# Causal mask of an attention stage moved from TensorE matmuls to GpSimd selections, and expert scatters issued between later gathers

## The reference

```python
xn = _layernorm(x)
x = x + L0_attn(xn, ...) + L0_ffn(xn, ...)          # block 0
xn = _layernorm(x)
x = x + L1_attn(xn, ...) + L1_ffn(xn, ...)          # block 1, a scan over segments of 32

# L0_attn: 16 heads of 8, no mask, scores scaled and multiplied by exp(-1e-4 |i - j|)
attn = softmax(clip(q k^T * scale) * decay); out = (attn v) Wo

# L0_ffn: a causal attention and a mixture of experts
scores = (rope(q) rope(k)^T) / sqrt(8)
scores = where(tril, scores, -inf)
x = x + (softmax(scores) v) w_o
logits = rmsnorm(x) @ w_router; top 2 of 8 experts; each expert keeps its 160 largest gates
xe = xf[tok]                                        # (8, 160, 128), gathered rows
ye = (relu(xe w1) w2) * gates
y = zeros.at[tok].add(ye)                           # rows added back
```

## Time and profile before

| | |
|---|---|
| three runs | 3370.74, 3374.51 (median), 3388.30 us |
| profiled execution | 3378.05 us, of which the profile's span is 3376.2 us |
| busy in the span | PE 2890.8 us, DVE 2501.5, ACT 1930.5, POOL 1697.3 |
| attend, from its first score matmul to its last division | 320.1 to 1525.1 us |
| experts, first gather issued | 1763.95 us |
| expert 0: transposition on PE starts, `ye` done on DVE | 1773.42, 1778.94 us |
| experts, last scatter issued | 1843.30 us |
| preparation of block 1 starts | 1851.1 us |

### The profile page before, as it was taken

One profiled execution on the slowest core, in us unless ns is written; L12 is line 12 of the kernel. 1 busy time (PEld: TensorE's weight loads), 2 busy tenths in 40 slices (PEclk: granted clock), 3 DMA queues, 4 the chain that ended last, 5 costly groups with the idle time before them and its releaser, 6 DMA issues. The chain is left out here.

```text
span 3376.2 us, 133974 instructions
## 1 busy us (share of the span) xinstructions
PE 2890.8 (86%) x56049; PEld 1694.1 (50%) x56049; DVE 2501.5 (74%) x7471; ACT 1930.5 (57%) x3909; POOL 1697.3 (50%) x1600
## 2 busy tenths in 40 slices
PE   5675999999999999997233299999999999999998
PEld 2332333333333333336222167676677767676776
DVE  4567788887888888866660678788888788787876
ACT  4564778787787878772000155555555555555553
POOL 4663000000000000003016499999999999898996
PEclk9777899999999999998565599999999999999999
DMA  3467333333233333309201200000000000000000
GB/s 123 169 207 231 70 83 85 89 77 87 75 85 84 87 87 76 87 25 286 82 27 29 74 4 11 11 11 11 11 11 11 11 11 11 10 7 9 11 7 11
DMA packets 179424, 210.31 MB, mean 62 GB/s; under 512 B 28608, under 2 KB 140288, under 8 KB 178560
## 3 DMA queue, kind: packets, MB, share of 16 engines
q1 hardware_dynamic: 176256, 200.31, 21.3%
q0 software_dynamic: 2560, 1.35, 0.4%
HBM read 125.17 MB, written 75.63 MB: 59 GB/s over the span
## 5 line engine op out<-in xcount | busy, mean ns | idle before, releaser
L778 ACT ACTIVATE at_pA<-at_ps 128x512 f32<-128x512 f32 x1024 | 569.1, 608 | 131.6 <-DVE at_ps L831 131.1
L840 DVE CUSTOM_DVE_ANT_0 at_junk<-at_ps,w_cmask 128x512 f32<-128x512 f32 (+3 forms) x1024 | 462.7, 488 | 169.9 <-PE at_ps L682 169.9
L658 POOL CAST at_mrow<-at_neg 16x128 bf16<-16x128 f32 x64 | 18.0, 282 | 1110.3 <-DVE at_neg L803 1110.3
L831 DVE TENSOR_TENSOR at_ps<-at_ps,w_ratio 128x128 f32<-128x128 f32 (+3 forms) x1024 | 490.4, 493 | 67.2 <-PE at_ps L676 67.0
L784 ACT ACTIVATE at_pB<-at_ps 128x512 f32<-128x512 f32 (+1 forms) x768 | 395.9, 538 | 77.3 <-PE at_ps L692 76.8
L2099 ACT ACTIVATE sc_ee<-sc_ps 128x512 f32<-128x512 f32 x256 | 153.0, 598 | 497.9 <-PE sc_ps L1955 496.5
L676 PE MATMUL at_ps<-at_aq,at_ak 72*128 72x512 bf16 x1024 | 355.9, 391 | 3.5 <-DMA at_ak<-parts_scratch 3.1
L1919 POOL TENSOR_TENSOR sc_rb<-sc_rb,v_sin 128x512 f32<-128x512 f32 x256 | 327.0, 1278 | 48.5 <-DVE sc_ra L2143 48.1
L682 PE MATMUL at_ps<-at_bk,at_bq 72*128 72x512 bf16 (+3 forms) x1024 | 273.2, 309 | 52.3 <-DMA at_bk<-parts_scratch 31.6
L1955 PE MATMUL sc_ps<-sc_xT,v_wqkv 128*128 128x512 f32 x512 | 293.1, 655 | 18.8 <-DVE sc_ra L2143 16.6
L689 PE MATMUL at_ps<-at_bq,at_bk 75*128 75x512 bf16 (+3 forms) x1024 | 283.3, 303 | 18.3 <-DVE at_mx L840 17.3
(11 more groups left out here) (315 smaller groups left out, 6377.9 us busy)
## 6 DMA issues: line engine op xcount, KB each, us to landing
parts_scratch<-fr_parts SPq DMA_DIRECT2D x64, 384.0 KB, 4.1
at_bq<-parts_scratch SPq DMA_DIRECT2D x192, 96.0 KB
at_bk<-parts_scratch SPq DMA_DIRECT2D x192, 96.0 KB
at_aq<-parts_scratch SPq DMA_DIRECT2D x192, 96.0 KB
at_ak<-parts_scratch SPq DMA_DIRECT2D x192, 96.0 KB
v_scratch<-fr_v SPq DMA_DIRECT2D x32, 352.0 KB, 4.3
at_v<-v_scratch SPq DMA_DIRECT2D x32, 352.0 KB, 3.5
parts_scratch<-fr_parts SPq DMA_DIRECT2D x32, 256.0 KB, 3.9
```

The lines of the kernel that those rows point to most:

```text
L778: act.activation(pA[:, n % A_RING, j * S:(j + 1) * S], src, ACT.Exp).then_inc(exped, 1)
L831: dve.tensor_tensor(src[:, 0:wide], src[:, 0:wide], W["ratio"][:, S - wide:S], ALU.mult).then_inc(tilted, 1)
L840: ins = dve.tensor_tensor_reduce(junk[:, P * j * (j + 1) // 2:P * (j + 1) * (j + 2) // 2], src[:, col:col + wide], W["cmask"][:, S - wide: ...
```

## The change

`attend`: the mask matmuls are gone, and each T block is one matmul. GpSimd instead zeroes the future keys in `pB` after the exponentials, with two in-place `affine_select` per head: one over the diagonal square of block 3 when T1's exponential is done, one over those of blocks 0, 1 and 2 (three squares, 384 columns) when T2's is done. A select keeps an entry where column - partition >= 0 and writes 0 elsewhere. PV of a T group waits for the semaphore `cut` of these instead of for `exped`. The splitting of the maxima stays on GpSimd, now in one stream with the selections.

`experts`: GpSimd issues the gathers of experts 0, 1, 2, then the scatters of expert 0, the gathers of 3, the scatters of 1, and so on; the scatters of 6 and 7 come last.

`fold_weights`: `cmaskT` isn't loaded, and two casts to bf16 are gone.

```diff
@@ fold_weights
-                 (W["ident"], c["ident"]), (W["hsum"], c["hsum"]), (cmaskT, c["cmaskT"]),
+                 (W["ident"], c["ident"]), (W["hsum"], c["hsum"]),
...
-            dve.tensor_copy(W["ident_bf"][:], W["ident"][:])
-            dve.tensor_copy(W["cmaskT"][:], cmaskT[:])
@@ attend, gpsimd
-                for n in range(GROUPS):
+                def split_max(n):
                     b = n % 2
                     pool.wait_ge(job_read, jseq["MT", "M", n] + 1)
...
+                def cut_future(n):
+
+                    probs = pB[:, n % T_RING]
+                    pool.wait_ge(exped, nth["exped", ("T1", n)])
+                    lone = probs[:, B_AT[3]:B_AT[3] + P]
+                    pool.affine_select(lone, lone, [[1, P]], ALU.is_ge, 0.0, base=0, channel_multiplier=-1).then_inc(cut, 1)
+                    pool.wait_ge(exped, nth["exped", ("T2", n)])
+                    three = bass.AP(probs.tensor, probs.offset, [list(probs.ap[0]), [S, 3], [1, P]])
+                    pool.affine_select(three, three, [[0, 3], [1, P]], ALU.is_ge, 0.0, base=0, channel_multiplier=-1).then_inc(cut, 1)
+
+                for e in range(STEPS):
+                    n = head_of("T", e)
+                    if n is not None:
+                        cut_future(n)
+                    if e % 4 == 0 and 0 <= e // 4 - 1 < GROUPS:
+                        split_max(e // 4 - 1)
+
@@ attend, tensor
                     for j, col in T_BLOCKS[kind]:
-                        pe.matmul(ps[:, BANK[kind], col:col + S - j * P], bk[:, slot, n % 4, j * P:(j + 1) * P], bq[:, slot, n % 4, j * P:S],
-                                  start=True, stop=False)
-
-                        ins = pe.matmul(ps[:, BANK[kind], col:col + P], W["ident_bf"][:], W["cmaskT"][:], start=False, stop=True)
+                        ins = pe.matmul(ps[:, BANK[kind], col:col + S - j * P], bk[:, slot, n % 4, j * P:(j + 1) * P], bq[:, slot, n % 4, j * P:S],
+                                        start=True, stop=True)
...
-                        pe.wait_ge(exped, nth["exped", (last_head[kind], 4 * g + 3)])
+                        if a == 0:
+                            pe.wait_ge(exped, nth["exped", ("A2", 4 * g + 3)])
+                        else:
+                            pe.wait_ge(cut, 2 * (4 * g + 3) + 2)
@@ experts, gpsimd
+            def fetch(e):
+                for m in (2 * e, 2 * e + 1):
+                    pool.indirect_dma_start(xe[0:HALF, m, :], None, c["xf_d"].rearrange("b s d -> (b s) d"),
+                                            bass.IndirectOffsetOnAxis(rows[0:HALF, m, 0:1], 0)).then_inc(fetched[e], 16)
...
+            def give_back(e):
                 pool.wait_ge(scaled, e + 1)
-
-                pool.wait_ge(summed, 32 * e)
...
+                if e:
+                    pool.wait_ge(summed, 32 * e)
+                for m in (2 * e, 2 * e + 1):
+                    pool.indirect_dma_start(c["h_d"].rearrange("b s d -> (b s) d"),
+                                            bass.IndirectOffsetOnAxis(rows[0:HALF, m, 0:1], 0), ye[0:HALF, m, :], None,
+                                            compute_op=ALU.add).then_inc(summed, 16)
+
+            for e in range(E):
+                fetch(e)
+                if e >= 2:
+                    give_back(e - 2)
+            for e in range(E - 2, E):
+                give_back(e)
```

More of the change, by code:

```diff
@@ L67, in fold_weights @@
         wqkv, wqkv_g, g1 = sb("fw_qkv", [P, 3 * D]), sb("fw_qkv_g", [P, 3 * D]), sb("fw_g1", [P, 1])
-        wq, cmaskT = sb("fw_q", [P, D]), sb("fw_cmaskT", [P, P])
+        wq = sb("fw_q", [P, D])
         ps = ctx.enter_context(nc.psum_tensor("fw_ps", [P, 4, 512], F32))
@@ L501, in attend @@
         pv, ot_cp, job, job_read, m_ready = (sem(n) for n in "pv ot_cp job job_read m_ready".split())
-        v_step, p_step, ones = (sem(n) for n in "v_step p_step ones".split())
+        v_step, p_step, ones, cut = (sem(n) for n in "v_step p_step ones cut".split())
         BANK = dict(A0=2, A1=4, A2=0, A3=1, M0=5, M1=4, M2=3, T0=5, T1=3, T2=2)
@@ L568, in attend @@
         LAST = 1 + max(e for (e, n), w in plan.items() if w)
-        last_head = {"A": "A2", "T": "T2"}
         with nc.Block() as block:
@@ L1469, in _ @@
         def _(pool):
[L1470 to L1476, removed]
-                pool.wait_ge(scaled, e + 1)
-                pool.wait_ge(summed, 32 * e)
-                pool.indirect_dma_start(c["h_d"].rearrange("b s d -> (b s) d"),
-                                        bass.IndirectOffsetOnAxis(rows[0:HALF, m, 0:1], 0), ye[0:HALF, m, :], None,
-                                        compute_op=ALU.add).then_inc(summed, 16)
+            def fetch(e):
+                for m in (2 * e, 2 * e + 1):
+                    pool.indirect_dma_start(xe[0:HALF, m, :], None, c["xf_d"].rearrange("b s d -> (b s) d"),
+                                            bass.IndirectOffsetOnAxis(rows[0:HALF, m, 0:1], 0)).then_inc(fetched[e], 16)
+                    pool.indirect_dma_start(ge[0:HALF, m, :], None, c["gate_d"],
+                                            bass.IndirectOffsetOnAxis(rows[0:HALF, m, 1:2], 0)).then_inc(fetched[e], 16)
+            def give_back(e):
+                pool.wait_ge(scaled, e + 1)
+                if e:
[10 more added lines that the diff above has]
+                give_back(e)
             pool.wait_ge(summed, 32 * E)
@@ L2247, in weights @@
     W = {n: sb(n, s) for n, s in shapes.items()}
-    W["ident_bf"], W["cmaskT"], W["flag"] = sb("ident_bf", [P, P], BF16), sb("cmaskT", [P, P], BF16), sb("flag", [1, 1], I32)
+    W["flag"] = sb("flag", [1, 1], I32)
     return W
@@ L2261, in shape_constants @@
     hsum = (np.arange(P)[:, None] % H == np.arange(H)[None, :]).astype(f32)
-    cmaskT = np.where(np.arange(P)[:, None] <= np.arange(P)[None, :], 0.0, MASKED).astype(f32)
     theta = (f32(10000.0) ** (f32(-2.0) * (np.arange(HD // 2, dtype=f32) / HD))).astype(f32)
@@ L2289, in shape_constants @@
     return dict(**route, **scan, ident=np.eye(P, dtype=f32), decay=decay, ratio=ratio, cmask=cmask,
-                hsum=hsum, cmaskT=cmaskT, rope=rope)
+                hsum=hsum, rope=rope)
 def inputs_of(a):
```

## The result

The changed kernel takes 3326.11 us (median of four runs, 3324.04 to 3332.28) against 3375.67 us before (3370.74 to 3388.30), a ratio of 0.9855, 95% interval 0.9835 to 0.9875. The forecast was 3321 us, range 3305 to 3350. The profiled execution took 3327.13 us, of which the span is 3325.4; before it was 3376.2, so 50.8 us are to be found.

A forecast was written before the change was run, and what follows sets the result against it. TensorE's own instruction stream was taken to bound most of each 18.44 us attention group. Terms - 43.8 + 0.9 - 10.2 - 0.7 = - 53.8 us took 3378.05 to 3324.2, or 3321 us by the median; range 3305 to 3350.

The forecast's parts named there:

- Masks: Attention: 12 of 16 mask matmuls per group count at 0.057 us, 0.684 us per group, 43.8 us over 64 groups.
- three chains: Attention: T0 awaiting M0's maximum, M0 awaiting T0's exponential, T1 awaiting M2's maximum swallow one, two and one masks per group.
- TensorE's two waits: Attention, once per group: 0.33 us for an exponential, 0.28 us for VectorE's maximum; to grow by 0.11 and 0.06 us.
- Selections: Attention, GpSimd: 1.0 to 1.5 us per head, 4 to 6 us per group, hidden except at the very end.
- The rival in which GpSimd is the bound: Attention: from about 7.8 ns per column GpSimd sets the group; at 8.6 ns 20.0 us, total 3466 us; chance 0.08.
- End of attend: Last group of attention: nothing stands between the last exponentials and their product, so the selection shows, + 0.9 us once.
- Experts: Experts stage, GpSimd: interleaved scatters no longer wait for earlier pairs; pair 7 starts at 1831.4 instead of 1841.59, - 10.2 us.
- Folding: Folding stage, ahead of its barrier: one DMA issue (0.43 us) and two casts (0.22 us) less, - 0.7 us.
- All masks: Rival, attention: all masks count, 58.4 instead of 43.8 us, as both waits shrink too; time 3306; chance 0.08.
- slack altogether: Rival, attention: masks are all slack, a loop over the banks sets the 18.44 us group; time 3364; chance 0.08.
- the half case: Rival, attention: new waits on banks not yet free take half of the 43.8 us, leaving 22; time 3343; chance 0.16.

## Why the prediction was right, and where it wasn't

- **Masks, - 0.684 us per group.** Measured - 0.65. The picture was right: TensorE's stream is the bound, each mask costs the distance of two starts, and a few are swallowed by three chains. The step that failed is the count, 12 of 16: it is 11. T2's mask of the third step was put among those that count because an unblocked matmul stands behind it, but it lies between M0's start and T1, in VectorE's chain of three maxima, whose length is fixed (2.63 us before, 2.64 after). The price per mask is 0.059 and not 0.057 us, as 0.65 / 11. 11 x 0.059 = 0.65, x 64 = 41.6 us.
- **TensorE's two waits** were to grow by 0.06 and 0.11 us: 0.06 and 0.12.
- **Selections.** 0.81 us per head where 1.0 to 1.5 was taken; 292 ns for 128 columns, at the lower end of the 0.3 to 0.5 that was to be seen, and 520 for 384, below the 0.6 to 1.0. Taking the streaming rows as the nearest was right in kind: (520 - 292) / 256 columns is 0.89 ns each, next to the memset's 0.86. GpSimd's share is 26%, in the range of a quarter to a half. No product waits for it in the steady state, and VectorE's 686 ns don't change. The rival in which GpSimd is the bound doesn't hold at four times these selections and does at five.
- **End of attend, + 0.9 us.** + 2.7 against the kernel without selections: the standstill is 0.6 us longer where 0.9 was taken, and the term that was missing is the granted clock, which fell behind the longer standstill; the product took 1.69 us more.
- **Experts, - 10.2 us.** - 9.3. The first pair came 15.14 us after the first gather (forecast 15.15) with a wait of 0.65 us for the product, and pair 7 at + 68.4 instead of + 67.4. The mis-sized term is the period of an expert, 8.26 us from 3.41 + 4.85: the first is 8.45 (1737.05 to 1745.50), since a pair of scatters takes 3.55 and the four gathers behind it 4.90, the first of them 1.25 instead of 1.21. The five periods take 42.06 us (1737.05 to 1779.11) where 41.3 was forecast, and two of 5.6 follow where 5.5 was taken: together the whole microsecond that is missing.
- **Folding, - 0.7 us.** The first load of `fr_x` behind this stage's barrier is issued at 15.85 us, before at 16.63: - 0.78. The start of attend moved by - 1.8; the other microsecond has no cause that was looked for.
- **Sum.** Terms as measured: - 41.6 + 2.7 - 9.3 - 0.8 = - 49.0 us, against - 50.8 by the spans and - 49.6 by the medians. By the spans attend lost 44.1, not 41.6 - 2.7 = 38.9, and the stretch behind it gained 3.9. Most of the 5.2 us between these lies at the start of the stage: from the first A score matmul to the third MT it is 58.45 us before (320.14 to 378.59) and 52.68 after (318.26 to 370.94), 5.8 less, of which the 20 masks there can be some 1.7 at most (11 at a distance of 0.11, 9 at 0.06); over the 60 groups behind it is 39.0 less, which is 60 x 0.65. The prediction had left the first groups' clock out. The 3.9 are open. These two were in no term and nearly cancel, so that the total came as close as the terms did is luck.
- **Rivals.** All masks (3306 us, a group under 17.6) and slack altogether (3364, 18.4) are excluded by 17.79. New waits do take a share, 5 masks of 16, but 4 of these were in the forecast: the half case falls.

## What to carry to other kernels

Before counting instructions taken off a bound engine, mark every chain that starts at one of its instructions and ends at a later one; what lies between them is slack, and such a chain can hide behind merged rows without idle time, so compare start to start. When the last waits of the bound engine are known, look at the order of the queue that feeds them: one swap on ScalarE, which wasn't the bound, gave 0.49 us per group, three quarters of what taking out 16 matmuls gave. The edge of a stage has less cover than its middle: an engine that keeps up in the steady state held TensorE up for 14 us in the last steps, once it had four times the selections to do.

## What was not expected of the hardware

A standstill of 1.55 us ahead of a product was followed by a fall of the granted clock, one of 0.96 us was not, and in the kernel with five times the selections one of 0.75 us was and one of 1.56 us wasn't. So the length of the standstill alone didn't decide it.

The moment at which the clock rises at the start of attend differs between two kernels with the same attention code, one execution each. Windows of the kernel before, and of the one with the experts' part alone (columns as in the earlier trace rows, the granted clock is the third number from the end):

```profile
340.00:350.00 10.00, 9.87 (x36) 1.40 (x34) 5.86 (x20) 4.41 (x8) 0.10 (x1) 0.50 0.62 124
350.00:360.00 10.00, 9.92 (x39) 3.51 (x36) 6.24 (x23) 5.00 (x10) 0.00 (x0) 0.50 0.24 60
360.00:370.00 10.00, 10.00 (x50) 4.33 (x49) 6.38 (x23) 6.47 (x13) 1.40 (x4) 0.60 0.01 1
```

```profile
340.00:350.00 10.00, 9.29 (x46) 1.96 (x50) 7.28 (x25) 4.54 (x9) 0.00 (x0) 0.78 0.55 120
350.00:360.00 10.00, 9.48 (x64) 3.76 (x56) 8.92 (x35) 9.04 (x19) 1.40 (x4) 1.00 0.19 44
```

TensorE is at the 1.2 GHz level for some 20 us longer in the first, though over 90% busy in both, and attend takes 1204.7 against 1196.7 us with the same group of 18.44. The same 8.0 us lie between the first A score matmul and the third MT (58.45 against 50.43), so they are the clock's. They are the reason why the group's length, and not the stage's, was compared throughout; the changed kernel's clock was at 0.82 already from 340 to 350 us, at 0.69 and 0.97 in the two windows behind, which fits an attend that lost 5.2 us more than the masks and the end explain.
